# Edge loop of a two-layer graph network: the turn of the last tile's silu rows placed first in TensorE's step

## The reference, cut to what matters

```python
def _mlp(x, W0, b0, W1, b1, g, b):
    h = silu(x @ W0 + b0)
    return _ln(h @ W1 + b1, g, b)
...
e = _mlp(mesh2grid_efeat, emb_W0, emb_b0, emb_W1, emb_b1, emb_g, emb_b)
e_in = concatenate([e, mesh_nfeat[src], grid_nfeat[dst]], axis=-1)
e_new = _mlp(e_in, edge_W0, edge_b0, edge_W1, edge_b1, edge_g, edge_beta) + e
agg = segment_sum(e_new, dst, num_segments=1250)
n_in = concatenate([grid_nfeat, agg], axis=-1)
n_new = _mlp(n_in, node_W0, node_b0, node_W1, node_b1, node_g, node_beta) + grid_nfeat
```

## Time and profile before

| what | value |
|---|---|
| median of three runs | 2556.91 us (2556.55 to 2559.67) |
| the profiled execution, its own time | 2557.4 us |
| its span in the trace | 2555.7 us |
| TensorE matmul busy over the span | 2279.1 us (89%) |
| TensorE weight load busy | 1928.7 us (75%) |
| VectorE, ScalarE, GpSimd busy | 1410.0 (55%), 1170.4 (46%), 1142.9 (45%) us |
| mean granted TensorE clock | 0.955 of full speed |

### The profile page before, as it was taken

One profiled execution on the slowest core, in us unless ns is written; L12 is line 12 of the kernel. 1 busy time (PEld: TensorE's weight loads), 2 busy tenths in 40 slices (PEclk: granted clock), 3 DMA queues, 4 the chain that ended last, 5 costly groups with the idle time before them and its releaser, 6 DMA issues. The chain is left out here.

```text
span 2555.7 us, 44732 instructions
## 1 busy us (share of the span) xinstructions
PE 2279.1 (89%) x13410; PEld 1928.7 (75%) x13413; DVE 1410.0 (55%) x3084; ACT 1170.4 (46%) x2117; POOL 1142.9 (45%) x1677
## 2 busy tenths in 40 slices
PE   2991288999988689999999999999999999999888
PEld 1430287777766578888888888888888888888776
DVE  7000297434344256666666666666666666666566
ACT  0210012232321156666666666666666666666521
POOL 4777400202020145555555555555555555555333
PEclk9996699999998889999999999999999999999989
DMA  6221001001012353233233233323232333323121
GB/s 184 78 68 19 14 0 37 11 27 37 1 36 75 101 145 63 60 61 63 59 64 59 63 60 62 62 57 66 57 65 58 62 61 59 64 59 64 30 89 42
DMA packets 76273, 149.57 MB, mean 59 GB/s; under 512 B 14690, under 2 KB 15790, under 8 KB 76220
## 3 DMA queue, kind: packets, MB, share of 16 engines
q0 software_dynamic: 44864, 93.18, 19.0%
q1 hardware_dynamic: 31243, 55.63, 6.6%
q10 hardware_dynamic: 112, 0.11, 0.0%
HBM read 129.12 MB, written 19.46 MB: 58 GB/s over the span
## 5 line engine op out<-in xcount | busy, mean ns | idle before, releaser
L1192 DVE CUSTOM_DVE_ANT_0 c_var_bank<-c_var_bank,c_p,k_floor 128x512 f32<-128x512 f32 x176 | 133.5, 758 | 369.6 <-PE c_var_bank L1349 369.6
L1083 POOL DMA_INDIRECT c_from_src<-s_dst_table,c_at_nodes x176 | 284.0, 1614 | 31.7 <-issue 31.7
L1403 PE MATMUL c_edge_bank<-c_m_hi,c_pt_hi 128*128 128x512 f32 x704 | 291.8, 414 | 0.0
L1404 PE MATMUL c_edge_bank<-c_m_lo,c_pt_hi 128*128 128x512 f32 x704 | 276.7, 393 | 0.0
L1405 PE MATMUL c_edge_bank<-c_m_hi,c_pt_lo 128*128 128x512 f32 x704 | 275.4, 391 | 0.0
L1077 POOL DMA_INDIRECT c_from_src<-s_mesh_table,c_at_nodes x176 | 206.4, 1173 | 150.7 <-POOL c_at_nodes L1073 141.9
L1089 POOL TENSOR_TENSOR c_dev<-c_var,k_half 128x1 f32<-128x1 f32 x176 | 98.1, 557 | 381.8 <-DVE c_var L1179 381.8
L1347 PE MATMUL c_var_bank<-c_m_hi,c_pt_hi 128*128 128x384 f32 x704 | 226.7, 322 | 4.7 <-ACT c_var_bank L1272 4.7
L263 POOL DMA_INDIRECT s_records<-a_stage_rec,a_stage_row x170 | 202.8, 1193 | 56.8 <-issue 48.7
L1347 PE MATMUL c_var_bank<-c_m_hi,c_ht_hi 128*128 128x384 f32 x704 | 226.1, 321 | 0.0
L1298 ACT ACTIVATE c_h<-c_from_src 128x512 f32<-128x512 f32 x176 | 111.2, 632 | 248.5 <-DVE c_from_src L1211 248.5
(11 more groups left out here) (298 smaller groups left out, 6097.9 us busy)
## 6 DMA issues: line engine op xcount, KB each, us to landing
k_w<-in_L_gnn_Ws_self_dram SPq DMA_DIRECT2D x3, 1024.0 KB
k_w<-in_L_gnn_Ws_neigh_dram SPq DMA_DIRECT2D x3, 1024.0 KB
c_from_src<-s_mesh_table,c_at_nodes POOLq DMA_INDIRECT x176
c_from_src<-s_dst_table,c_at_nodes POOLq DMA_INDIRECT x176, 4.7
s_records<-a_stage_rec,a_stage_row POOLq DMA_INDIRECT x170
a_mesh<-in_L_gnn_mesh_nfeat_dram SPq DMA_DIRECT2D x10, 250.0 KB
k_h<-in_x_dram SPq DMA_DIRECT2D x1, 2500.0 KB
s_mesh_table<-a_mesh_out SPq DMA_DIRECT2D x10, 250.0 KB
```

What stands on the lines that cost most here:

```text
L1083: pool.indirect_dma_start(from_src[u][:], None, scratch["dst_table"], bass.IndirectOffsetOnAxis(ap=at_nodes[u][:, 1:2], axis=0), compute_o ...
L1192: dve.tensor_tensor_reduce(var1_bank[:], var1_bank[:], p[u % 2][:], 1.0 / D, k["floor"][:, 0:1], ALU.mult, ALU.add, var[u][:, 0:1]).then_i ...
L1403: pe.matmul(edge_bank[:], left[0], m_hi[1][:, c, :], start=False, stop=False, skip_group_check=True)
L1404: pe.matmul(edge_bank[:], left[0], m_lo[1][:, c, :], start=False, stop=False, skip_group_check=True)
```

## The change

Three statements of TensorE's step move. Transposes of tile n-1, and in step `u == 2` the wait for `attr_t_ok` that guards `turn_bank`, now stand first in the step, before the features of tile n+1. They stood behind the feature rows of n+1 and before the edge matmuls of n. Nothing is added or removed, and no other engine's order is touched.

```diff
         def step(i, v, u):
             n = GROUP * i + u
             after = 1 - v if u == GROUP - 1 else v
+            if u == 2 and exists(n + 2):
+                pe.wait_ge(attr_t_ok, i + 2)
+            if exists(n - 1):
+                turn_h(n - 1, (u - 1) % 4)
             if u == GROUP - 1 and exists(n + 1):
                 pe.wait_ge(attr_t_ok, i + 2)
             if exists(n + 1):
@@
             if exists(n + 1):
                 feature_rows(n + 1, after, (u + 1) % 4)
-            if u == 2 and exists(n + 2):
-                pe.wait_ge(attr_t_ok, i + 2)
-            if exists(n - 1):
-                turn_h(n - 1, (u - 1) % 4)
 
             pe.wait_ge(edge_set, n + 1)
```

## The result

The changed kernel takes 2634.56 us (median of six runs, 2630.04 to 2636.01) against 2557.12 us for the kernel before (six runs): a ratio of 1.030, 95% interval 1.0287 to 1.0313. It is slower by 77 us. The profiled execution took 2635.63 us, 78.2 more than the one of before.

A forecast was written before the change was run, and what follows sets the result against it. TensorE looked busy throughout, but variance2 waits for VectorE's `ht_lo`, tied to the square's end. Terms 77 + 6 - 4 = +79 on the profiled 2557.4 give 2636.4, with the median 0.5 lower: 2636 us, range 2613 to 2664.

The forecast's parts named there:

- `ht_lo` hangs on the square's end: Between square and variance2: VectorE's 3.08 us run from the square's end sets `ht_lo`; earlier transposes can't make it earlier.
- Front and back would cancel in TensorE's own work: Four transposes: 0.44 us saved behind the square, 0.44 added ahead of it, cancelling by TensorE's own work.
- The 77 us term: Ahead of the square: 0.44 us counts in full in 175 steps, as variance2 still waits for `ht_lo`: +77 us.
- Bucket ends, +6: At nine bucket ends transposes wait about 0.93 us for `h`, +8; part already paid at the feature rows goes: +6.
- `h` in the fourth steps is early enough: Head of every fourth step: `h`, 0.17 us late by the old rows, should end 0.27 early; cost taken as nothing.
- What eases, -4: At variance2: late loads average 0.20 us against 0.13 shown, through late `h` in fourth steps; about half of 8 goes.
- Rival 4, the clock: In the loop: pauses of 0.44 us lower TensorE's clock, adding 105 us, to 2741 us; chance 4%.

The follow-up runs named there:

- run 1: Changed kernel with two VectorE instructions swapped, the remainder `ht_lo` made before `pt_lo`: 2560.03 us, 1.0015 times the kernel before.
- run 4: Changed kernel with the transposes moved directly behind the square, ahead of the feature rows: 2557.06 us, ratio 1.0002 to the kernel before.
- run 5: Changed kernel with two matmuls of zeros (512 columns) added ahead of the edge matmuls, behind the square: 2635.82 us.
- run 6: Kernel before with two matmuls of zeros added ahead of the square, transposes in their old place: 2625.21 us, ratio 1.0265.
- run 10: Changed kernel with `ht_lo` before `pt_lo` and `leave` first in VectorE's step, on the same chip as run 8: 2544.73 us, ratio 0.9952.
- run 8: Kernel before, transposes in the old place, with `ht_lo` before `pt_lo` and `leave` first in VectorE's step: 2553.93 us, ratio 0.9987.
- run 7: Changed kernel with `leave` (copy and clearing of the sums at a bucket end) first in VectorE's step: 2624.52 us.

## Why the prediction was right

2636 us was predicted and 2634.56 measured, with the mechanism named.

- **`ht_lo` hangs on the square's end.** Right: 3.45 us to the load of variance2 in the step shown of both kernels, 3.52 in both on average. Runs 1 and 4 to 6 show it: the cost goes when VectorE's list is reordered, or when the transposes pass the square, and comes when other work passes it the other way.
- **Front and back would cancel in TensorE's own work.** Nearly right: the front took 0.40, not 0.44, and the back freed 0.46 of TensorE's own time (3.09 to 2.63 up to the last edge load). That the back frees more than the front takes shows in run 10 against 8, as 9 us. The wait became longer than forecast by the same count: 0.20 + 0.46 = 0.66. The 77 us term measured 70 (175 x 0.40). I had priced transposes by the features' pace of 0.11 per load; they came at 0.097 (0.39 / 4). The Trainium skill's 81 ns per pair, from "TensorE: Matmul & The Clock Gate", section Back-to-back issue gap, would have given 57 as an estimate: the trace lies between.
- **Bucket ends, +6.** Measured +7 (9 x 0.75). The cause, `leave` ahead of `z`, is borne out by run 7.
- **`h` in the fourth steps is early enough.** Right: between 1000 and 2400 us only three weight loads beside the bucket ends waited for `h` (1.1, 0.3 and 0.3 us). At the longest of them `h` was unusually late in the kernel before too, 1.15 us behind the end of the step. POOL's lateness shrank as said; `h` came 0.15 us ahead of the end of the step where it had been 0.16 behind.
- **What eases, -4.** Wrong. In those fourth steps `low_ht` still ends 0.10 us later than in others (3.50 us after the square's last matmul, 3.51 before), although `h` is no longer late. So late `h` wasn't its cause. In both kernels the 0.10 lies between the small bound and `low_rh`, which starts 1.35 us after the feature rows' load instead of 1.25, while its input from ScalarE is ready at 0.72 in all four places; it arises on VectorE, and why stays open. The term should have been 0. The errors of -7, +1 and +4 cancel for the most part, and so the time came out closer than its terms: that is luck. The rest of the 78 lies ahead of the first tile's sums.
- **Rival 4, the clock.** It did not happen in the changed kernel (1.00 in the loop). I had set it aside because pauses are short. Run 1 shows pauses as short as 0.91 and 0.78 us, 2 us apart, followed by the lower level at eight of nine places. In the same run one pause alone of 1.15 us (at 1838.8) was not, and in the changed kernel pauses of 0.2 to 0.3 us in nearly each step were not. The Trainium skill's sentence in the same page, section The HAM clock gate, that activity releases a throttle which is the default, agrees with these drops in direction.

## What to carry to other kernels

TensorE was recorded 99.8% busy here and yet had no slack against another engine: look at how late its weight loads are, and at which event the waited-for list starts. Moving work from behind that event to ahead of it cost its full length here, though TensorE's own work balanced. The move that lost 77 us gained 9 once two neighbouring instructions on VectorE had changed places, so try a move again after the wait that ate it is gone.

## What the runs showed of the hardware that was not expected

Two pauses of TensorE of 0.91 and 0.78 us, 2 us apart, were followed by a granted clock of 0.50 for about 3 us, and a cost of 1.5 us, at eight of nine places in run 1. At the ninth, pauses of 0.91 and 0.85 us were followed by no drop, so the pauses alone don't settle it; what else does was not tested. In the changed kernel, with pauses of 0.3 to 0.5 and about 0.8 us at the same nine places, the clock is 1.00 and the steps show no such loss. Four transposes of 32-bit rows took 0.39 us for their loads where four loads of rounded weights took 0.45 (1464.21 to 1464.66); why was not tested.
